# Two-layer graph network on one core: reordering the seam between the two diffusion steps

## What is computed

```python
Rf = S / rowsum(S);  Rb = S / colsum(S)       # S = adj + eye
for s in range(2):
    logits = (Xa @ W1) @ W2 @ (Xa @ W3).T
    keep = the largest logits of each row until their softmax mass reaches 0.9
    A = softmax(where(keep, logits, -inf))
    Xf, Xb, Xa = Rf @ Xf, Rb @ Xb, A @ Xa
    Z = Z + Xf @ U1[s] + Xb @ U2[s] + Xa @ U3[s]
out = x + layernorm(h + Z) * gamma + beta
```

## Time and profile before

| | us |
|---|---|
| median of three runs | 2220.41 |
| the profiled execution | 2220.01 |
| its span in the profile | 2218.3 |
| VectorE busy | 1940.6 (87%) |
| TensorE busy | 1896.4 (85%) |
| ScalarE busy | 1683.4 (76%) |
| GpSimd busy | 665.4 (30%) |

### The profile page before, as it was taken

One profiled execution on the slowest core, in us unless ns is written; L12 is line 12 of the kernel. 1 busy time (PEld: TensorE's weight loads), 2 busy tenths in 40 slices (PEclk: granted clock), 3 DMA queues, 4 the chain that ended last, 5 costly groups with the idle time before them and its releaser, 6 DMA issues. The chain is left out here.

```text
span 2218.3 us, 32410 instructions
## 1 busy us (share of the span) xinstructions
PE 1896.4 (85%) x9866; PEld 1262.6 (57%) x9866; DVE 1940.6 (87%) x6109; ACT 1683.4 (76%) x1740; POOL 665.4 (30%) x1366
## 2 busy tenths in 40 slices
PE   1999954999999999999863989989888989899882
PEld 1555532666666666666641656565655666565662
DVE  6777788899998999999748999999999999999995
ACT  4334345999999999999626898988888888989840
POOL 2000042334444343344504223232323222322214
PEclk9999976999999999999986999999999999999996
DMA  6777521011111111111126010101010010101023
GB/s 220 280 286 285 199 97 48 30 55 54 36 51 54 54 50 54 55 55 43 45 67 210 1 44 22 44 22 44 22 44 23 29 37 22 44 22 44 21 92 119
DMA packets 65725, 167.61 MB, mean 76 GB/s; under 512 B 7037, under 2 KB 45307, under 8 KB 61947
## 3 DMA queue, kind: packets, MB, share of 16 engines
q1 hardware_dynamic: 65530, 165.43, 21.5%
HBM read 117.95 MB, written 47.45 MB: 75 GB/s over the span
## 5 line engine op out<-in xcount | busy, mean ns | idle before, releaser
L1438 PE MATMUL banks<-xa,pt 128*128 128x256 f32 x2704 | 640.7, 388 | 5.0 <-ACT pt L943 4.3
L1438 PEld LDWEIGHTS banks<-xa,pt 128*128 128x128 f32 x2704 | 506.6, 194 | 144.5 <-issue 71.3
L914 ACT ACTIVATE junk_a<-pb_all,minus_t 128x3327 f16<-128x3327 f32 x150 | 461.0, 3073 | 93.2 <-POOLq L841 90.5
L919 ACT ACTIVATE junk_a<-pb_all,minus_t 128x3327 f16<-128x3327 f32 x150 | 460.6, 3071 | 4.1
L1489 PE MATMUL banks<-region,at 128*128 128x512 f16 x2028 | 456.6, 380 | 0.0
L826 POOL TENSOR_SCALAR over<-over,points 128x1 f32<-128x1 f32 x150 | 124.0, 827 | 839.4 <-ACT junk_a L919 839.4
L1489 PEld LDWEIGHTS banks<-region,at 128*128 128x128 f16 x2028 | 196.5, 98 | 218.5 <-issue 2.7
L1364 PE MATMUL banks<-keys,qs 64*128 64x512 f32 (+1 forms) x816 | 190.6, 567 | 98.3 <-DMA qs<-q_d 32.2
L1430 PE MATMUL banks<-ident,pb_all 128*128 128x128 f32 x1352 | 196.1, 296 | 53.0 <-DVE pb_all L1161 51.9
L943 ACT ACTIVATE pt<-banks 128x896 f32<-128x896 f32 x208 | 172.4, 858 | 88.7 <-PE banks L1430 88.7
L1230 DVE TENSOR_SCALAR_CACHE_REDUCE pb_all<-banks 128x1024 f32<-128x1024 f32 x260 | 209.2, 848 | 27.5 <-PE banks L1364 19.1
(11 more groups left out here) (222 smaller groups left out, 2756.5 us busy)
## 6 DMA issues: line engine op xcount, KB each, us to landing
at<-adjT_d SPq DMA_DIRECT2D x52, 832.0 KB, 4.9
region<-in_adj_dram SPq DMA_DIRECT2D x25, 1663.5 KB, 8.0
adjT_d<-at SPq DMA_DIRECT2D x26, 832.0 KB, 3.9
fb_d<-fb_sb SPq DMA_DIRECT2D x26, 256.0 KB, 2.0
region<-fb_d SPq DMA_DIRECT2D x2, 3328.0 KB, 19.4
y_d<-y_sb SPq DMA_DIRECT2D x50, 128.0 KB, 1.7
x_d<-pb_all SPq DMA_DIRECT2D x1, 3328.0 KB, 10.4
qs<-q_d SPq DMA_DIRECT2D x104, 32.0 KB, 4.1
```

Of the source, the lines that this page charges most:

```text
L914: nc.scalar.activation(junk_a[:, 0:w], pb[u][:, 0:w], ACT.Relu, scale=sign, bias=t, accum_out=over[u][:, 0:1])\
L919: nc.scalar.activation(junk_a[:, 0:w], pb[u][:, 0:w], ACT.Sign, scale=sign, bias=t, accum_out=over[u][:, 1:2])\
L1438: last = nc.tensor.matmul(bank[4][:, 0:D], pt[sl][:, t * P:(t + 1) * P], xa[:, t0 + t, :], start=(t0 + t == 0), stop=(t0 + t == T - 1))
```

## The change

1. **Last tile of step one.** Tile 25 has two levels on ScalarE and GpSimd instead of three (`LEVELS[0][T - 1] = LAST_BISECTIONS = 2`), and two bisections on VectorE instead of one.
2. **Keys first.** ScalarE copies the keys before the queries and signals them alone (`k_done`); for tile 25, PE turns its Xa before Xf and Xb, computes queries and keys and the last logits of tile 0, and only then multiplies with U. ScalarE copies the queries and keys of tile 25 right behind the turned Xf and Xb.
3. **Coarse search** of tile 0 of step two moves from VectorE's end of step one to its start of step two, behind the barrier and ahead of `take_logits` of tile 1.
4. **Loads of `fb_d`.** 25 of 26 tiles are loaded by SyncE in step one, in its body i = T, behind a wait for all sparse products of step one and for the stores of tiles 0 to 24, and ahead of the four stores of tile 25. The last tile is loaded behind the barrier.
5. **Queries** in step two are loaded four tiles ahead instead of three, and those of tile 2 ahead of U, `fb_d` and `xa_d`.

```diff
+    LEVELS[0][T - 1] = LAST_BISECTIONS = 2
@@ SyncE
-                    for ahead in ((2, 3) if i.static and i.t == -2 else (3,)):
+                    for ahead in ((2, 3) if first and i.t == -2 else (3, 4) if i.t == -2 else (3,) if first else (4,)):
...
-                        for h in range(2):
-                            hs = slice(h * T // 2, (h + 1) * T // 2)
-                            sp.dma_start(parts_fb[:, hs, :], fb_d[hs].rearrange("t p c -> p t c")).then_inc(S("fb_loaded"), 16)
+                        sp.dma_start(parts_fb[:, T - 1, :], fb_d[T - 1]).then_inc(S("fb_loaded"), 16)
...
+                    if first and i.t == T:
+                        sp.wait_ge(S("sx_psum"), T)
+                        for u in range(2):
+                            sp.wait_ge(S2("fb_stored")[u], 16 * (T // 2 - u))
+                        for hs in (slice(0, HT), slice(HT, T - 1)):
+                            sp.dma_start(parts_fb[:, hs, :], fb_d[hs].rearrange("t p c -> p t c")).then_inc(S("fb_loaded"), 16)
                     if first and k.inside(T):
@@ ScalarE
-                        act.wait_ge(S("z_psum"), q.n + 1)
+                        act.wait_ge(S("qk_psum"), q.n + 1)
+                        nc.scalar.activation(key_tiles(1, q.t, 1), bank[7][DA:2 * DA, D:D + P], ACT.Copy).then_inc(S("k_done"), 1)
                         act.wait_ge(S("qo_stored"), 16 * q.n)
-                        nc.scalar.activation(qo[:, :], bank[7][0:DA, D:D + P], ACT.Copy)
-                        nc.scalar.activation(key_tiles(1, q.t, 1), bank[7][DA:2 * DA, D:D + P], ACT.Copy)\
-                            .then_inc(S("qk_done"), 1)
+                        nc.scalar.activation(qo[:, :], bank[7][0:DA, D:D + P], ACT.Copy).then_inc(S("qk_done"), 1)
...
+                    if first and k.t == T - 1:
+                        own_turned(k)
                     if k.inside(T):
                         act.wait_ge(S("fbT_psum"), k.n + 1)
...
-                    if first and k.inside(T):
+                    if first and k.inside(T) and k.t < T - 1:
                         own_turned(k)
+                    if first and k.t == T - 1:
+                        queries_keys(k)
@@ VectorE
+                    if first and i.t == T - 1:
+                        AB = LAST_BISECTIONS
...
+                        if not first and i.t == -2:
+                            coarse_search(i + 2)
                         spread(i + -1)
+                        if first and i.t == T + 1:
+                            take_logits(nxt, 3, NL)
                         add_z(i + -2)
                         if first and i.t == T:
                             take_logits(nxt, 0, 3)
-                        if first and i.t == T + 1:
-                            take_logits(nxt, 3, NL)
-                            coarse_search(nxt)
@@ TensorE
+                        if first and k.t == T - 1:
+                            pe.wait_ge(S("fbT"), k.n + 1)
+                            queries_keys(k)
+                            logits_ahead(len(LCH) - 1)
+                            pe.wait_ge(S("qk_done"), T)
```

30 lines of the change are left out of this document (16 added, 14 removed).

## The result

The changed kernel took 2225.32 us (median of 20 runs, 2222.77 to 2227.47), the kernel before 2220.72 us in the same job (20 runs, 2219.01 to 2223.31). The ratio is 1.0020 with a 95% interval of 1.0013 to 1.0026: **slower by 4.6 us**. Forecast were 2219.0 us, 2213.5 to 2223.5. The profiled execution took 2226.93 us, of which 2225.2 lie in its span.

What follows compares the result with a forecast made beforehand. Step two was taken to run at VectorE's pace, so only the seam, about 1080 to 1260 us, could move. Terms -3.1 + 1.8 = -1.3 us gave 2218.7 profiled, 2219.0 us as median, range 2213.5 to 2223.5.

Steps and rivals of the forecast that it cites:

- Step 1: Last tile of step one: VectorE begins 8.2 us earlier, pays 4.16 us for one more bisection, net 4.1 us earlier.
- the clock as a rival: Within "No hold" (chance 0.15): TensorE's 0.50 clock slows the sparse product, delays tile 0's mask and keeps the old phase.
- Step 2: Barrier between the steps: stores queue behind two large loads issued at 1128.2, so it opens at 1149.0, 6.2 us earlier.
- Step 3: Coarse search behind the barrier: tile 1's logits complete 10.0 us behind it instead of 6.9, 3.1 us later.
- Step 4: Early queries in step two: PE's wait goes, search 1 starts 2.9 us earlier, yet VectorE ends 1.8 us later.
- The held level: Tile 2's second rough level: GpSimd's last instruction starts inside VectorE's pass at 1216.6 and is held to 1220.4.
- the second hold: GpSimd's third level of tile 2 is held by VectorE's next pass, 1222.1 to 1225.8, then takes 1.6 us.
- the old phase: Behind tile 1's search in step two, the mask covers GpSimd's last level again, and no more is lost.
- the third pair: Search of tile 1: VectorE waits some 0.7 us more for PE's third pair, behind PE's product.
- The sum: Whole kernel: 3.1 us earlier at step two's start plus 1.8 us later in tile 1's search, -1.3 us.
- The late loads: Rival, chance 0.08: loads at 289 GB/s or less hold the barrier to 1154.7 or later; 2229 us at 242 GB/s.
- No hold: Rival, chance 0.15: GpSimd's levels slip between VectorE's passes or the old phase stays; 2.9 us kept, 2214.4 us.

Runs made afterwards that it cites:

- Run 2: Kernel before with only the last-tile edit of step one, plus 22 thrown-away products in PE's gap before the last sparse product: 2216.43 us, ratio 0.9979.
- run 9: Changed kernel plus 22 thrown-away products in PE's gap before the last sparse product of step one: 2223.75 us, ratio 1.0013 to the kernel before.
- run 1: Kernel before with only the last-tile edit of step one (two levels, two bisections): 2218.17 us, ratio 0.9989.
- run 8: Changed kernel without early loads of `fb_d`, with 22 thrown-away products in step one and VectorE's wait in tile 1's search: 2211.37 us, ratio 0.9958 to the kernel before.
- run 4: Changed kernel where VectorE, before its second pass of tile 1 in step two, waits for GpSimd's second rough level of tile 2: 2219.32 us, ratio 0.9995.
- run 10: Changed kernel with both the 22 thrown-away products in step one and VectorE's wait in tile 1's search: 2218.30 us, ratio 0.9991 to the kernel before.
- run 3: Kernel before with only the queries change (tile 2's ahead of the large loads, then four tiles ahead): 2224.16 us, ratio 1.0019.
- run 5: Kernel before with only the coarse search of step two moved behind the barrier: 2221.34 us, ratio 0.9999.
- run 6: Kernel before with only the early loads of `fb_d`, issued right behind the store of tile 24: 2224.63 us, ratio 1.0018.
- run 7: Changed kernel with its coarse search moved back ahead of the barrier: 2223.08 us, ratio 1.0010 to the kernel before.
- run 12: Run 8 plus 14 thrown-away products (6 and 8) in PE's two gaps in the last tile of step two: 2210.80 us, ratio 0.9959 to the kernel before.

## Why the prediction was wrong

**Step 1, "Net 4.1 us earlier, for everything up to SyncE's store of tile 24", is the step that failed.** The changed kernel shows 0.5 us at the transposes of tile 25. VectorE's own part of the sum came to 3.2 us instead of 4.1. The rest was lost on PE. The prediction itself said that PE "still waits for VectorE's `add_z` before the last sparse product", and took idle PE time as free. PE's 5.34 us gap lets its granted clock fall, and 26 products of 5.78 us take 8.36. Run 2 puts the clock's share at 2.5 us; run 9 finds the same in the changed kernel (34.9 against 37.6 from the mask of tile 24 to the transposes). The prediction used the clock as a rival at one place, the sparse product behind the queries, and not at the place where its own change made a gap.

"TensorE: Matmul & The Clock Gate" in the Trainium skill, Part 1, says that the slow level is the default and that activity releases the fast one, and that the clock's trace events show these two levels only. The rows agree: groups of equal products come at 5.78 us, or longer where the stretch's mean clock is lower. What this gap costs here is read from runs 1, 2 and 9.

**Step 2, the barrier.** 6.2 us earlier were forecast; 1.3 came. The loads left 4.4 us later than the 1128.2 assumed, 3.8 by the distance from the mask of tile 24, which is step 1. From their issue to the barrier the forecast had 20.8 us; it took 21.8, and 22.9 in run 9. The arrangement was right: stores wait behind loads, at 386 GB/s once the flow is full. The two terms that were estimates without a row, 1.5 us for the start and 0.9 for the end, were too small: in the changed kernel the windows show 267 and 338 GB/s from 1134 to 1138, and 1.2 us pass from the end of the flow to the barrier, 2.4 in run 9.

**The clock in step one is not the whole miss.** Run 9 has the clock back and still opens its barrier at 70.8 against 67.5 forecast, and starts search 1 at 133.5 against 129.8. Of the 4.9 us missed at the barrier the repair returns 1.6, of the 4.3 at search 1 it returns 0.6. The 3.7 left in run 9 are the 0.9 us on VectorE, 0.2 on the way to the loads' issue, 2.1 from there to the barrier, and some 0.4 behind it. That hangs on the order itself: without the loads ahead of the stores (run 8) search 1 is at 127.3.

**Step 3.** 10.0 us from barrier to logits were forecast (the terms named, 4.9, 4.6 and 0.3, add up to 9.8), 9.4 measured, 10.3 in runs 4, 9 and 10. Right within that. Keys first was called a single copy of 0.3 us; it brings the end of the exponentials 2.8 us nearer to the transposes of tile 25 (27.5 us behind them instead of 30.2), which the loads hide, as the prediction had it.

**Step 4.** The held level, its place (the pass of search 1, though its third instruction and not its last), the second hold, VectorE's wait (3.8 forecast, 3.95 measured) and the return to the old phase all came. The sum from search 1 to search 2 was 4.7 us and measured 6.3: the term of 0.7 us for the third pair is 2.33, since PE's ten products ran in 3.88 instead of 2.43 us. The clock a second time, behind a gap of 3.52 us.

**The sum.** Forecast to last mask -1.3, measured +3.8. Between lie 4.3 us at search 1, from steps 1 and 2 as above, and 1.6 us in the search, less 0.8 us that step two regained later. The end adds between 0 and 2.5 us by execution; with the median up 4.6 us and the last mask 3.8 later in the one profiled execution, that fits, but the mean share of the end isn't shown.

**The rivals.** The late loads were given 0.08 and a threshold: from a barrier at 1154.7 on, +4.4 us. It opened at 1154.4, with +4.6. The number came out by that rival's bookkeeping and not by its mechanism, for the flow was 386 GB/s and not under 289. I had tied lateness to the rate of the flow alone, not to the time of issue, and so gave too little chance to the slow side. "No hold" stood at 0.15, on a margin of 0.4 us. Runs 4 and 10 show that the hold costs 5.5 to 6.0 us. The margin of 0.4 us was right and is firm. In the six profiles that show the hold (changed kernel, runs 3, 5, 6, 7, 9) GpSimd's third instruction begins 0.01 to 0.02 us behind the pass, which itself begins 2.21 to 2.22 us behind the start of search 1. The fourth follows the third by 0.38 us where nothing holds it (run 4), so it would still begin 0.4 us inside the pass if the third slipped out. There VectorE waits for GpSimd (3.19 us above, 1.57 us in run 5), so both engines start from one event, and the lengths of their instructions fix the rest.

## What to carry to other kernels

An edit that shortens one engine's wait opens a gap on another: where that other is TensorE and the gap grows from about 1 to 5 us, count what its clock loses behind it (here 2.5 of 3.2 us), and test it with products that are thrown away. Removing a wait in a pipeline whose engines block each other may cost more than the wait did (5 us removed, 3.9 us lost), and a small wait at the right place can be worth 5.5. Two good edits can exclude each other: moving work behind a barrier gained 2.6 us at the next logits by itself (run 5) and cost 2 once a load set ahead of the stores held the barrier (run 7).

## What the runs showed of the hardware

- A gap of 5.3 us in front of 26 products of 128x512 f16 stretched them from 5.78 to 8.22 (run 1) and 8.36 us (changed kernel), but to 7.29 in run 4's execution and 6.75 in run 7's: the same gap costs 1.0 to 2.6 us by execution.
- The GpSimd instruction that begins 0.02 us behind the start of VectorE's 3.68 us pass took 3.74 us instead of 0.28 in six kernels. A VectorE that starts 0.86 us later, by a wait, gets 5.5 to 6.0 us back.
- The last stores, issued behind 6.5 MB of loads, landed late: in the changed kernel the last issue at 1146.37 was followed by 8.0 us of waiting at the barrier; without the loads ahead it was 3.5 us in run 8 (from 1142.44 to 1145.93) and 2.2 us in run 12 (from 1142.90 to 1145.06).
